# Loading x one piece at a time, and four semaphores for the first weight quarters, in an attention and feed-forward kernel on eight cores

## The chip, the cores and the metric

One Trainium2 chip, all eight of its cores. The batch has eight sequences and each core computes one of them by itself; the cores exchange nothing. The metric is the device time of the slowest core in microseconds. "Faster", "same" and "slower" go by a bound of 2%.

## The reference

```python
def _layernorm(x, axis=-1, eps=1e-5):
    m = jnp.mean(x, axis=axis, keepdims=True)
    v = jnp.var(x, axis=axis, keepdims=True)
    return (x - m) / jnp.sqrt(v + eps)

def attn(x, Wq, Wk, Wv, Wp):                 # 16 heads of 64, D = 1024
    q, k, v = x @ Wq, x @ Wk, x @ Wv         # split into heads
    scores = jnp.einsum('bnhk,bmhk->bhnm', q, k) / sqrt(64)
    out = jnp.einsum('bhnm,bmhv->bnhv', softmax(scores), v)
    return x + out @ Wp

def ffn(x, weight, aux_weight1, aux_weight2, bias):
    return jnp.tanh(x @ weight @ aux_weight1 @ aux_weight2 + bias)

x = x + attn(_layernorm(x), Wq, Wk, Wv, Wp)  # x: (8, 2048, 1024) f32
x = x + ffn(_layernorm(x), weight, aux_weight1, aux_weight2, bias)
```

## The kernel before

The host hands each core its sequence transposed, x as [1024, 2048] f32. On the chip `xr` holds it as eight chunks (j = 0 to 7) of 128 features by 2048 tokens, f32, 8 MB in all. The matrices are f32 in memory and are used as bf16; each is cut into four quarters of 256 output columns. A quarter is read as 1 MB of f32, cast on its way and written as 512 KB of bf16. GpSimd (POOL) issues these loads (`preload_head_quarters`, L170 to L175, and `issue_wdma`, L130 to L138). SyncE (SP) issues the loads of x (L210 to L212) and, much later, the stores of the result (L714). The two kinds of transfer thus stand in two queues, q0 for POOL and q1 for SP, and are moved by the same 16 DMA engines.

The work goes in stages.

1. Start. SP loads two identity matrices and the bias. All engines wait for these. POOL issues ten quarters in a row: the four of wq and the four of wk into the eight slots of `vt`, which is not needed for anything else yet, and the first two of wv into `wbuf`. SP issues four loads of x, 2 MB each, two chunks to a load: load jj fills chunks 2jj and 2jj + 1 and has a semaphore of its own, `d_x[jj]`.
2. Statistics of the first layer norm (L226 to L239). For each chunk VectorE (DVE) waits for its `d_x`, casts the chunk to bf16 (L231) and squares it (L233); TensorE (PE) then adds up values and squares over the features with eight matmuls against ones, four on `ln_mean` (L236) and four on `ln_sq` (L239). Casts use two buffers in turn, so a cast also waits for the matmuls of the chunk two before it.
3. When the last of these matmuls is done, DVE forms mean and variance over [128, 2048] (L244, L246, L248), ScalarE (ACT) takes Ln and Exp (L251, L253), and for each chunk DVE subtracts, multiplies and adds back (L261, L267, L271) while ACT casts the result to `S` (L269) and PE multiplies it with the first quarter of wq (L277).
4. Projections q and k (L327), v with transposes (L368, L392), a bound for the exponents (L424), and then the long attention loop, into which the output projection and the feed-forward network are woven.

A matmul that uses one of the first eight quarters (`use_wquarter`, L149 to L152) waits for a semaphore in `d_wh`. There are two of them: quarters 0, 2, 4, 6 count on the first and 1, 3, 5, 7 on the second, and the wait asks for all four of its semaphore.

```python
        for jj in range(4):
            d_x[jj].inc(SP.dma_start(xr_j[:, 2 * jj:2 * (jj + 1), :], xsrc[jj]))
...
                    if dma_gate:
                        VE.wait_ge(d_x[j // 2].h, 16)
                    if j >= 2:
                        VE.wait_ge(s_te.h, mm_mark[sl])
                    m1 = s_ve.inc(VE.tensor_copy(xbf[sl], src_f32_j[:, j, :]))
```

Of the kernel before, what the change touches and what calls it, by code (L numbers as in the profile page):

```python
# [51 lines left out]
def build_program(upto=99, dbg=False):  # L52
    nc = bass.Bass("TRN2", target_bir_lowering=False)
# [17 lines left out]
    E = ctx.enter_context  # L71
    with ctx:
# [32 lines left out]
        d_x = [DSem(E(nc.semaphore(f"d_x{i}"))) for i in range(4)]  # L105
        d_w = [DSem(E(nc.semaphore(f"d_w{i}"))) for i in range(NWS)]
        d_wf = [DSem(E(nc.semaphore(f"d_wf{i}"))) for i in range(6)]
        d_wh = [DSem(E(nc.semaphore(f"d_wh{i}"))) for i in range(2)]
        d_o = [DSem(E(nc.semaphore(f"d_o{i}"))) for i in range(2)]
        d_misc = DSem(E(nc.semaphore("d_misc")))  # L110

        TE, VE, SE, SP, GP = nc.tensor, nc.vector, nc.scalar, nc.sync, nc.gpsimd
# [15 lines left out]
        def wslot(s):  # L128
            return wbuf[:, 2048 * s: 2048 * (s + 1)].rearrange("p (i d) -> p i d", i=8)
# [10 lines left out]
        def vtslot(k):  # L140
            return vt.ap()[:, 2048 * k: 2048 * (k + 1)].rearrange("p (i d) -> p i d", i=8)
# [4 lines left out]
        def flslot(k):  # L146
            return kbslot(k) if k < 6 else vtslot(k - 6)

        def use_wquarter(idx):  # L149
            if idx < 8:  # L150
                TE.wait_ge(d_wh[idx % 2].h, 16 * 4)
                return vtslot(idx)  # L152
            if idx >= FLUSH_W0:
                k = idx - FLUSH_W0
                s = FL_SEM[k]
                nf = sum(1 for ss in FL_SEM if ss == s)
                TE.wait_ge(d_wf[s].h, 16 * nf)
                return flslot(k)
            s = idx % NWS
            nloads = sum(1 for i in range(8, idx + 1) if i % NWS == s)  # L160
            TE.wait_ge(d_w[s].h, 16 * nloads)
            return wslot(s)
# [7 lines left out]
        def preload_head_quarters():  # L170
            for k in range(8):
                wn, q = wq_order[k]
                src = w_d[wn].rearrange("(i p) d -> p i d",
                                        p=128)[:, :, 256 * q: 256 * (q + 1)]
                d_wh[k % 2].inc(GP.dma_start(vtslot(k)[:], src))  # L175

        def _fl_load(k):
            wn, q = wq_order[FLUSH_W0 + k]
# [20 lines left out]
        for e in (TE, VE, SE, SP):  # L199
            e.wait_ge(d_misc.h, d_misc.n)  # L200
        preload_head_quarters()
        issue_wdma(8)
        issue_wdma(9)
# [5 lines left out]

        xsrc = x_d.rearrange("(jj q p) n -> jj p q n", p=128, q=2)  # L210
        for jj in range(4):
            d_x[jj].inc(SP.dma_start(xr_j[:, 2 * jj:2 * (jj + 1), :], xsrc[jj]))  # L212

        def layernorm(src_f32_j, dst_bf16, add_back, dma_gate=False, wq0=False):
# [7 lines left out]
            with nc.psum_tensor(_nm("ln_mean"), [128, 2048], F32) as mps, \  # L222
# [31 lines left out]
                VE.wait_ge(s_se.h, m)  # L254
            def _normalize(wq0_pj):
                wsl0 = use_wquarter(0) if wq0_pj is not None else None
                mkq0 = 0
                for j in range(NCH):
# [49 lines left out]
        def wproj(widx0, src_bf, dst_bf, q0=0, ev_init=None):  # L308
            with nc.psum_tensor(_nm("pj0"), [128, 2048], F32) as p0, \
                 nc.psum_tensor(_nm("pj1"), [128, 2048], F32) as p1:  # L310
                pj = [p0, p1]
                ev_mark = [0, 0]
                first = True
                for q in range(q0, 4):
                    widx = widx0 + q
                    wsl = use_wquarter(widx)
                    for jj in range(2):
                        j = 2 * q + jj
                        sl = j % 2
                        if first and ev_init is not None:  # L320
                            TE.wait_ge(s_se.h, max(ev_init))
                        first = False
                        if ev_mark[sl]:
                            TE.wait_ge(s_se.h, ev_mark[sl])
                        for i in range(NCH):
                            for n4 in range(4):
                                ins = TE.matmul(  # L327
                                    pj[sl][:, 512 * n4:512 * (n4 + 1)],
                                    wsl[:, i, 128 * jj:128 * (jj + 1)],
                                    src_bf[:, 2048 * i + 512 * n4: 2048 * i + 512 * (n4 + 1)],  # L330
                                    start=(i == 0), stop=(i == NCH - 1))
                        mk = s_te.inc(ins)
                        SE.wait_ge(s_te.h, mk)
                        ev_mark[sl] = s_se.inc(SE.copy(dst_bf[:, 2048 * j:2048 * (j + 1)],
                                                       pj[sl][:]))
                        if jj == 1:
                            done_wquarter(widx, mk)
# [8 lines left out]
        with nc.psum_tensor("pva", [128, 1024], F32) as pva, \  # L346
# [11 lines left out]
            for q in range(4):  # L358
                widx = 8 + q
                wsl = use_wquarter(widx)  # L360
                for jj in range(2):
                    j = 2 * q + jj
# [502 lines left out]
def _get_nc():  # L865
    if "nc" not in _NC_CACHE:
        _NC_CACHE["nc"] = build_program()
    return _NC_CACHE["nc"]
# [31 lines left out]
```

## Time and profile before

| | us |
|---|---|
| median of 2 runs | 1317.65 (1317.57 to 1317.73) |
| the profiled execution, its own time | 1320.32 |
| its span, slowest core (core 1) | 1318.7 |
| spans of the eight cores | 1305.1 to 1318.7 |
| PE busy | 1009.0 (77%) |
| ACT busy | 723.9 (55%) |
| DVE busy | 413.2 (31%) |

The span runs from the first to the last instruction of one core. The profile shows the slowest core, core 1; the run's own time is 1.6 us more than its span, which lies around it. All times of the trace are counted from the span's start. Engines are PE, PEld (weight loads of PE), DVE, ACT, POOL and SP; a "q" behind a name means its sequencer, which issues transfers. A packet is one piece that a DMA engine moves; bytes are counted as written, so a weight quarter counts 512 KB.

### The profile page before, as it was taken

The numbers are of one execution on the slowest core, as the hardware profiler recorded it, in microseconds if no ns is written. First come the engines' busy times: TensorE is split into PE (matmuls) and PEld (weight loads), VectorE is DVE, ScalarE is ACT, GpSimd is POOL, SyncE is SP. The second block draws the span as 40 slices with busy tenths as digits, with TensorE's granted clock in tenths as the row PEclk, the third lists the DMA queues.
The fourth block names the chain that finished last, engine by engine and source line by source line (L and its number), as shares of the span: only waits on it lengthen the run. The fifth ranks groups of instructions, "written<-read, shape, count | busy, mean of one in ns | idle before, by whom it ended". The sixth has DMA issues, their size and how long they took to land.

```text
span 1318.7 us, 15346 instructions; the slowest of 8 cores (1305.1 to 1318.7 us)
## 1 busy us (share of the span) xinstructions
PE 1009.0 (77%) x5185; PEld 334.8 (25%) x5185; DVE 413.2 (31%) x542; ACT 723.9 (55%) x686; POOL 66.8 (5%) x80
## 2 busy tenths in 40 slices
PE   2345999886677777787997678799777879977676
PEld 1111444442122222222332222233222223322222
DVE  3596000345701101234222223522222342222354
ACT  0122222004588898298668729866872986677202
POOL 2000000000000000100110010011001001111100
PEclk9665999996599999899998889999888999988879
DMA  9900000121000000500453340045335004593901
GB/s 239 175 1 0 0 0 1 17 33 16 0 1 0 1 1 1 64 1 1 60 70 65 64 64 1 1 57 72 56 70 68 1 1 51 67 160 58 145 0 64
DMA packets 85113, 57.65 MB, mean 44 GB/s; under 512 B 2088, under 2 KB 79920, under 8 KB 84016
## 3 DMA queue, kind: packets, MB, share of 16 engines
q0 software_dynamic: 79040, 39.85, 24.6%
q1 hardware_dynamic: 6000, 16.82, 3.7%
q8 instruction: 46, 0.75, 0.2%
q14 instruction: 27, 0.22, 0.1%
HBM read 88.12 MB, written 8.39 MB: 73 GB/s over the span
## 4 chain that ended last, share of the span: by engine, by line
PE 43%; ACT 16%; DVE 6%; issue 5%; DMA 2%; ACTq 0%; DVEq 0%; POOLq 0%
ACT S L760 14%; PE sc L526 10%; PE pvs L772 9%; PE dns L782 6%; PE lnps L674 4%; PE wps L674 4%; PE wps L548 2%; PE lnps L692 2%; DMA wbuf<-wp 2%; PE lnps L548 2%; PE wps L692 1%; DVE S L793 1%; DVE S L795 1%; DVE S L655 1%; DVE vtmp L652 1%
## 5 line engine op out<-in xcount | busy, mean ns | idle before, releaser
L760 ACT ACTIVATE S<-sc,cbias 128x1024 bf16<-128x1024 f32 x512 | 550.9, 1110 | 191.7 <-PE dns L785 178.7
L526 PE MATMUL sc<-qb,kb 64*128 64x512 bf16 x512 | 202.1, 395 | 116.2 <-ACT S L760 106.9
L772 PE MATMUL pvs<-S,vt 128*64 128x512 bf16 x512 | 214.4, 419 | 25.9 <-DVE S L795 25.9
L777 PE MATMUL pvs<-S,vt 128*64 128x512 bf16 x512 | 215.1, 420 | 0.0
L530 PE MATMUL sc<-qb,kb 64*128 64x512 bf16 x512 | 206.1, 403 | 0.0
L785 PE MATMUL dns<-S,ones 128*64 128x512 bf16 x512 | 204.6, 400 | 0.0
L782 PE MATMUL dns<-S,ones 128*64 128x512 bf16 x512 | 204.5, 399 | 0.0
L526 PEld LDWEIGHTS sc<-qb,kb 64*128 64x128 bf16 x512 | 47.6, 93 | 342.2 <-issue 342.2
L327 PE MATMUL pj<-S,vt 128*128 128x512 bf16 x448 | 98.7, 384 | 6.3 <-ACT qb L294 3.9
L772 PEld LDWEIGHTS pvs<-S,vt 128*64 128x64 bf16 x512 | 55.1, 108 | 150.4 <-issue 150.3
L793 DVE COPY S<-pvs 128x512 f32<-128x512 f32 x32 | 22.1, 691 | 189.5 <-PE dns L785 189.5
L424 ACT ACTIVATE S<-qb 128x2048 bf16<-128x2048 bf16 x8 | 15.1, 1906 | 81.9 <-PEq L402 78.4
L327 PEld LDWEIGHTS pj<-S,vt 128*128 128x128 bf16 x448 | 44.1, 99 | 61.3 <-issue 9.8
L785 PEld LDWEIGHTS dns<-S,ones 128*64 128x64 bf16 x512 | 57.5, 112 | 0.0
L782 PEld LDWEIGHTS dns<-S,ones 128*64 128x64 bf16 x512 | 57.4, 112 | 0.1
L138 POOL DMA_DIRECT2D wbuf<-w x36 | 31.5, 874 | 510.1 <-PE sc L530 451.4
L777 PEld LDWEIGHTS pvs<-S,vt 128*64 128x64 bf16 x512 | 55.1, 108 | 0.0
L382 DVE CAST vtmp<-pva 128x1024 bf16<-128x1024 f32 x8 | 9.8, 1225 | 135.4 <-PE pva L368 135.4
L277 PE MATMUL pq0a<-S,vt 128*128 128x512 bf16 x32 | 14.9, 620 | 45.5 <-ACT S L269 45.5
L530 PEld LDWEIGHTS sc<-qb,kb 64*128 64x128 bf16 x512 | 47.6, 93 | 0.0
L548 PE MATMUL wps<-S,wbuf 128*128 128x512 bf16 x104 | 31.1, 453 | 20.5 <-DMA wbuf<-wp 15.1
L705 ACT ACTIVATE S<-S,bias_pp_sb 128x512 bf16<-128x512 bf16 x32 | 23.1, 722 | 37.2 <-DVE S L700 37.1
(153 smaller groups left out, 1123.8 us busy)
## 6 DMA issues: line engine op xcount, KB each, us to landing
wbuf<-w POOLq DMA_DIRECT2D x36, 512.0 KB, 6.2
xr<-x SPq DMA_DIRECT2D x4, 2048.0 KB, 24.0
out<-xr SPq DMA_DIRECT2D x32, 256.0 KB, 2.2
wbuf<-wp POOLq DMA_DIRECT2D x14, 512.0 KB, 6.4
vt<-w POOLq DMA_DIRECT2D x8, 512.0 KB, 20.0
vt<-wq POOLq DMA_DIRECT2D x4, 512.0 KB, 34.5
vt<-wk POOLq DMA_DIRECT2D x4, 512.0 KB, 48.6
wbuf<-wv POOLq DMA_DIRECT2D x4, 512.0 KB, 30.9
```

Of the source, the lines that this page charges most:

```text
L327: ins = TE.matmul(pj[sl][:, 512 * n4:512 * (n4 + 1)], wsl[:, i, 128 * jj:128 * (jj + 1)], src_bf[:, 2048 * i + 512 * n4: 2048 * i + 512 * ...
L526: TE.matmul(scs[sl][:, 0:512], kb[0:64, 2048 * p + 128 * m: 2048 * p + 128 * (m + 1)], qb[0:64, 2048 * p + 512 * c: 2048 * p + 512 * (c + 1)],
L530: ins = TE.matmul(scs[sl][:, 512:1024], kb[64:128, 2048 * p + 128 * m: 2048 * p + 128 * (m + 1)], qb[64:128, 2048 * p + 512 * c: 2048 * p ...
L548: ins = TE.matmul(acc[:], wsl[:, i, 128 * jj:128 * (jj + 1)], ao[:, 512 * i:512 * (i + 1)], start=(i == 0), stop=(i == NCH - 1))
L674: ins = TE.matmul(acc[:], wsl[:, i, 128 * jj:128 * (jj + 1)], rhs_of(i), start=(i == 0), stop=(i == NCH - 1))
L692: ins = TE.matmul(acc[:], wsl[:, i, 128 * jj:128 * (jj + 1)], h2st[:, 512 * i:512 * (i + 1)], start=(i == 0), stop=(i == NCH - 1))
L760: ins = SE.activation(p_un[sl], scs[sl][:], AF.Exp, bias=cbias[:], scale=0.125)
L772: TE.matmul(pvs[0:64, :], vt[:, 1024 * m + 128 * p: 1024 * m + 128 * p + 64], p_un[sl][:, 0:512], start=(m == 0), stop=(m == NM - 1), tile ...
L777: TE.matmul(pvs[64:128, :], vt[:, 1024 * m + 128 * p + 64: 1024 * m + 128 * (p + 1)], p_un[sl][:, 512:1024], start=(m == 0), stop=(m == NM ...
L782: TE.matmul(dns[0:64, :], ones64[:], p_un[sl][:, 0:512], start=(m == 0), stop=(m == NM - 1), tile_position=(0, 0), skip_group_check=True)
L785: ins = TE.matmul(dns[64:128, :], ones64[:], p_un[sl][:, 512:1024], start=(m == 0), stop=(m == NM - 1), tile_position=(0, 64), skip_group_ ...
L793: pv_evac_mark = s_ve.inc(VE.tensor_copy(ao_un, pvs[:]))
```

## The change

SP now waits, before it issues load jj of x, until load jj - 1 has landed. And the first eight quarters of weights count on four semaphores in place of two: quarter 0 alone on the first, quarter 1 alone on the second, 2, 4, 6 on the third and 3, 5, 7 on the fourth. No transfer, no instruction and no size is changed, and nothing changes its place on its engine.

```diff
-        d_wh = [DSem(E(nc.semaphore(f"d_wh{i}"))) for i in range(2)]
+        d_wh = [DSem(E(nc.semaphore(f"d_wh{i}"))) for i in range(4)]
+        WH_SEM = [0, 1, 2, 3, 2, 3, 2, 3]
...
         def use_wquarter(idx):
             if idx < 8:
-                TE.wait_ge(d_wh[idx % 2].h, 16 * 4)
+                s = WH_SEM[idx]
+                nh = sum(1 for ss in WH_SEM if ss == s)
+                TE.wait_ge(d_wh[s].h, 16 * nh)
                 return vtslot(idx)
...
-                d_wh[k % 2].inc(GP.dma_start(vtslot(k)[:], src))
+                d_wh[WH_SEM[k]].inc(GP.dma_start(vtslot(k)[:], src))
...
         for jj in range(4):
+            if jj:
+                SP.wait_ge(d_x[jj - 1].h, 16)
             d_x[jj].inc(SP.dma_start(xr_j[:, 2 * jj:2 * (jj + 1), :], xsrc[jj]))
```

SP's whole queue before, with what each entry waits for (`d_misc` counts the three small loads, `s_ve` is DVE's counter):

```order
L193 DMA identb_sb<-identb 128x128 [waits barrier_Pool_Activation_PE_DVE_SP_release]
L194 DMA identf_sb<-identf 128x8
L195 DMA bias_st<-bias 8x128
L212 DMA xr<-x 128x2x2048 [waits d_misc]
L212 DMA xr<-x 128x2x2048 x3
L714 DMA out<-xr 128x512 [waits barrier_Pool_Activation_PE_DVE_SP_release,s_ve]
L714 DMA out<-xr 128x512 [waits s_ve] x31
```

And after the change (lines are five further down):

```order
L196 DMA identb_sb<-identb 128x128 [waits barrier_Pool_Activation_PE_DVE_SP_release]
L197 DMA identf_sb<-identf 128x8
L198 DMA bias_st<-bias 8x128
L217 DMA xr<-x 128x2x2048 [waits d_misc]
L217 DMA xr<-x 128x2x2048 [waits d_x0]
L217 DMA xr<-x 128x2x2048 [waits d_x1]
L217 DMA xr<-x 128x2x2048 [waits d_x2]
L719 DMA out<-xr 128x512 [waits barrier_Pool_Activation_PE_DVE_SP_release,s_ve]
L719 DMA out<-xr 128x512 [waits s_ve] x31
```

The three last loads of x, which followed the first at once, each wait now for the one before them. On POOL, PE, DVE and ACT the rows are the same and stand in the same order.

## Rows read from the trace of the kernel before

**Rows 1.** The eight cores: span and mean granted clock; three of them.

```profile
core 1: 1318.7 us, clock 0.903
core 3: 1305.1 us, clock 0.913
core 7: 1306.0 us, clock 0.914
```

**Rows 2.** Timeline, 0 to 50 us: start, duration, instruction, idle time and its releaser.

```profile
4.50 2.96 SPq L212 DMA_DIRECT2D xr<-x  x4
...
8.64 1.83 POOL L138 DMA_DIRECT2D wbuf<-wv  x2
...
18.96 1.23 DVE L231 CAST qb<-xr 128x2048 bf16<-128x2048 f32 x1 [13.90 <-DMA xr<-x]
...
25.94 1.23 DVE L231 CAST qb<-xr 128x2048 bf16<-128x2048 f32 x1 [1.96 <-DMA xr<-x]
...
32.84 1.23 DVE L231 CAST qb<-xr 128x2048 bf16<-128x2048 f32 x1 [1.87 <-DMA xr<-x]
...
41.06 1.23 DVE L231 CAST qb<-xr 128x2048 bf16<-128x2048 f32 x1 [3.20 <-DMA xr<-x]
```

**Rows 3.** Timeline, 50 to 130 us.

```profile
50.43 2.29 DVE L244 TENSOR_SCALAR qb<-ln_mean 128x2048 f32<-128x2048 f32 x1 [4.35 <-PE ln_sq L239]
...
63.00 2.29 DVE L261 TENSOR_TENSOR qb<-xr,qb 128x2048 f32<-128x2048 f32 x1 [5.48 <-ACT qb L253]
...
69.83 1.86 PE L277 MATMUL pq0a<-S,vt 128*128 128x512 bf16 x4 [19.51 <-ACT S L269]
...
118.54 2.29 DVE L271 TENSOR_TENSOR xr<-xr,kb 128x2048 f32<-128x2048 f32 x1
...
128.01 7.24 PE L327 MATMUL pj<-S,vt 128*128 128x512 bf16 x25 [3.87 <-ACT qb L294]
```

**Rows 4.** The head's eight weight loads (L175): from issue to landing.

```profile
L175 POOL DMA_DIRECT2D vt<-wk x4: 923/938/950, 5.2 to 7.8; - x4
...
DMA to landing us min/median/max: 8.4/43.0/52.8
```

**Rows 5.** DMA queues, 20 to 26 us: packets, MB, share of 16 engines.

```profile
q1 hardware_dynamic: 246, 1.88, 90.6%
q0 software_dynamic: 243, 0.12, 14.9%
```

**Rows 6.** DMA queues, 46 to 54 us.

```profile
q0 software_dynamic: 2424, 1.22, 131.0%
```

**Rows 7.** Loads of x: who waited for them, and from issue to landing.

```profile
  DMA xr<-x: 20.9, 4
...
DMA to landing us min/median/max: 14.4/24.0/34.4
```

**Rows 8.** DMA queues, 4 to 8 us, and then 8 to 10 us.

```profile
q0 software_dynamic: 841, 0.43, 108.2%
...
q0 software_dynamic: 550, 0.27, 119.9%
q1 hardware_dynamic: 9, 0.07, 13.9%
```

**Rows 9.** Stores (L714), three stretches: 920 to 940, 1160 to 1180, 1212 to 1250 us.

```profile
DMA to landing us min/median/max: 2.2/2.2/2.2
...
DMA to landing us min/median/max: 6.1/6.4/6.7
...
L714 SPq DMA_DIRECT2D out<-xr x1: 332/332/332, 1218.8 to 1218.8; - x1
...
DMA to landing us min/median/max: 8.5/8.5/8.5
```

**Rows 10.** DMA traffic, 1218 to 1228 us in 40 slices of 0.25 us.

```profile
GB/s 14 25 80 174 197 195 186 184 197 195 180 162 123 139 123 145 160 184 123 80 139 178 217 264 299 252 240 205 203 193 115 148 166 152 147 135 131 131 147 180
```

**Rows 11.** Stages by time: PE busy (count), granted clock, DMA share, GB/s.

```profile
26.00:36.00 10.00, 5.57 (x26) 1.00 1.05 311
36.20:39.60 3.40, 3.40 (x10) 0.51 1.02 252
43.70:50.40 6.70, 6.56 (x16) 0.55 1.29 150
```

**Rows 12.** Longest waits of PE, 0 to 130 us: in total, times, longest.

```profile
PE pq0a L277 <- ACT S L269: 45.5, 8, 19.5
PE ln_mean L236 <- DVE qb L233: 24.2, 5, 16.9
```

**Rows 13.** Longest waits of SP's queue, whole span.

```profile
SPq L711 <- DVE xr L710: 946.9, 32, 337.5
```

## The prediction

> **What bounds the kernel now.** The change touches only the first 60 us, so I read the page for the whole, the list of cores, and then the timeline of the head, asking of each wait what ended it.
>
> The list of cores [rows 1] shows that the slowest core, 1, has the lowest granted clock (0.903); core 3, at 0.913, is 13.6 us shorter. That is the noise of size in this kernel, and the change has no direct hold on it.
>
> In the timeline DVE's casts L231 are the ones to look at. SP issues the four loads of x together at 4.50 us [rows 2]. DVE sits idle for the first until 18.96, and then again for the second, third and fourth: the casts start at 18.96, 25.94, 32.84 and 41.06, each with "DMA xr<-x" as releaser. So DVE waits for every load; the arrival of x sets the pace, and the intervals are 6.98, 6.90 and 8.22 us, 22.1 in all. Behind the last landing everything is a chain: statistics of two chunks until 50.43, mean and variance on DVE, Ln and Exp on ACT, the first subtraction at 63.00, the first projection matmul at 69.83, for which PE had waited 19.51 us [rows 3]. DVE's last operation of this chain is at 118.54, and no engine has other work it could do first. What is lost before 41.06 is therefore lost at the end, microsecond for microsecond.
>
> The weights are not on this chain. The last of the eight quarters is issued at 7.8 us and lands at most 52.8 us later [rows 4], at about 60.6, which is 9 us before PE first needs any of them, and then PE is released by ACT's cast, not by a DMA [rows 12].
>
> How do the two queues share the engines? Between 20 and 26 us, 246 packets of q1 (x) and 243 of q0 (weights) are moved: one for one, 1.88 MB against 0.12 [rows 5]. x has 313 GB/s and nearly the whole machine. When x is done, q0 alone moves 2424 packets in 8 us, 303 per us against 40 before [rows 6].
>
> The Trainium skill ("DMA: Bandwidth & Descriptors", section "Queues, rings and completion order") says that each engine takes turns between its queues packet by packet. By that rule, which these counts bear out, the big packets of x win whenever the queue of x is not empty. It would put the loss from the change in the times when that queue is empty, which is also what the rows below say.
>
> **The change part by part.**
>
> *The semaphores of the first quarters.* Before, the first projection matmul waits for quarters 0, 2, 4 and 6, now for 0 alone. All had landed 9 us earlier, so nothing is freed: 0 us. If x comes later, the matmul comes later too and the margin grows; the weights' own end moves by a few us at most (below). Both ends of this edit are 0; the cover is the late cast on ACT. The next quarters are used only from 128 us on [rows 3].
>
> *The waits on SP.* Three new waits. Behind the waiting instruction on SP stand only the next loads of x, and the stores, of which the first is issued at 694 us after SP has waited 337.5 us for DVE [rows 13]. So the waits hurt nobody but x itself. POOL issues from its own queue and doesn't see them.
>
> What a wait costs x: before, when an engine had moved its part of load jj, the packets of load jj + 1 stood behind it. Now its queue is empty until (a) all 16 engines have finished, (b) the semaphore has reached SP, (c) SP has issued the next load and its first packets come up. The price is the whole time from issue to landing of a load that starts into an empty queue, less the interval of a load that follows another. I look for rows of such a start.
>
> - The first load of x is one: same size, same queue, weights running beside it. Issued 4.50, landed after 14.4 us [rows 7]. And the queue rows show where that goes: from 4 to 8 us not one packet of q1, though issued; from 8 to 10 only 9, beside 550 of the weights [rows 8]. Some 4.8 us pass before x moves.
> - Stores of 256 KB, also on SP's queue. In a quiet stretch 2.2 us from issue to landing; beside a long row of weight loads 6.1, 6.7 and 8.5 [rows 9]. The slices show the last one: issued at 1218.79, and traffic rises above all that the weights had alone (197 GB/s) only in slices 23 to 27, from about 1223.5 on [rows 10]. Again about 4.7 us before the first packets.
>
> So two different transfers agree: with weights on the engines a start into the empty queue takes some 4.6 us to the first data. Add the 6.9 to 8.2 us of interval that a load needs once it flows, and 0.6 for the landing to be told (an estimate: a quiet store's 2.2 less 0.9 of data at 300 GB/s is 1.3, half of it ahead of the data and half behind). That is 12.1 to 13.4 us, and the whole first load says 14.4. I take 13.2, the middle of 12.1 and 14.4.
>
> Will weights be there in every gap? They have ten quarters, 5.24 MB, to write; by 19 us some 0.9 is done (0.43 and 0.27 to 10 us [rows 8], then 0.02 MB per us beside x [rows 5]). Each gap gives them about 4.6 us at 0.15 MB per us [rows 6], 0.7 MB, and each load leaves them about 0.2. At the third gap about 2.7 MB are done. They are still there, and end near 70 us (58.6 plus the last 1.6 MB at 0.15), the eighth quarter near 63.
>
> Sum: 3 x 13.2 = 39.6 us in place of 22.1, so x is complete 17.5 us later, at about 58.6. Does something absorb it? The pairs of chunks are 14 us apart instead of 7, and their 16 matmuls need 6.6 us at half speed [rows 11]; they are no bound. The last two chunks need 9.4 us behind the landing as before; their matmuls ran at a granted clock of 0.55, mostly the lower of the two levels. At full speed the 16 matmuls would end about 2 us sooner, but PE will have been idle longer before them than now, so I give it 0. The work behind is unchanged. On the profiled execution 1320.3 + 17.5 = 1337.8; the median of the runs is 2.7 us below the profiled time, so I predict 1317.65 + 17.5 = 1335.2.
>
> A bound below: quiet stores, 1.3 us of start and landing per load, +3 x 1.3 = +4, or -0 if a load has no uneven end any more. A bound above: 14.4 each, +21.1. Beyond it the longest store (8.5 against 2.2, +6.3 on top of 1.3) gives 6.9 + 7.6 = 14.5, the same.
>
> **The rivals.**
>
> *A quiet start.* The slow first start may belong to the start of the program, when POOL is still issuing loads (until 10.5 us [rows 2]) and all cores begin at once. Then a restart costs what a quiet store shows, 1.3 us, up to 2.2 if issue and landing hide nothing: +4 to +7, 1322 to 1325. For it: 9 packets come up just when POOL stops. Against it: the stores at 1168 and 1176 us, when POOL had long stopped issuing, also took 6 to 7 us.
>
> The Trainium skill (same page, section "Anatomy of one DMA") gives a fixed cost of about 2.0 us per DMA. By that rule the change costs 3 x 2.0 = 6 us and the time is 1323.7; the 2.2 of the quiet store agrees, the loaded stores do not.
>
> *Not slower at all.* Between 36 and 40 us x slows to 252 GB/s [rows 11], since some engines have finished their parts and others not. At 18.96 us some packets of load 2 have already gone, which the waits keep from load 1. If one load at a time has the engines evenly, each lands perhaps 1 us sooner, which pays the 1.3 us of a quiet restart, and with the last 16 matmuls at full clock 2 us come on top: 1316 to 1318. It decides where load jj + 1 lands within 7.4 us of load jj. Both must hold, a quiet restart and the gain; no row shows the second, so it is unlikely. It is also the case in which the waits do nothing, because the loads are taken in turn anyway.
>
> *Slower by over 2%*, over 1344.0. It needs +26.4 us: 14.4 per load (+21.1) and 5 us more, which a mean clock lower by 0.004 gives (13.6 us per 0.010, rows 1). Later x would have to change the clock of the attention; I see no path but chance, or a restart slower than the first.
>
> **How the numbers follow.** My forecast (restart beside running weights, +14 to +21.5) 0.70; quiet start 0.16; not slower 0.06; over 2% slower 0.07; and 0.01 for over 2% faster. 2% is about what a measurement of this kernel can tell from no change, and the forecast of 1.3% lies inside it: faster 0.01, same 0.92, slower 0.07. The range: my case with its spread (0.2% between the profiled execution and the median) reaches from 1329 to 1342; to leave no more than 2 in 10 out I take most of the quiet start in, from 1322.
>
> **What would show it.** In the changed kernel's timeline SP's loads of x stand apart, issued within 1 us of each landing. Casts of even chunks start at about 19, 32, 45 and 58.6 us; L244, 5 lines further down, at 68 in place of 50.4; the first projection matmul at about 87. DVE's wait for xr grows from 20.9 us in total [rows 7] to about 38. In the gaps the weights' packets rise to 300 per us, and the weights end near 70 us. From the last landing on, distances are as before. Wrong if the intervals are under 9 us (quiet start), if the first load lands clearly before 18, if PE waits for a DMA at the first projection, or if the head is as forecast and the end is not, which would put the time in the clock.

## The result, and the profile after

The changed kernel takes 1340.24 us (median of 11 runs) beside 1318.73 us for the kernel before (10 runs on the same chips). The ratio is 1.0153, with a 95% interval of 1.0124 to 1.0181: 16 to 24 us longer, about 20. It was forecast 17.5 us longer. In some runs of either kernel the cores of a die have a lower clock and take some per cent longer; the medians take these runs in, the ratios and the times of single runs leave them out. By the bound of 2% that is "same", and by the interval it is clearly slower.

The profiled execution has a span of 1336.0 us on core 0, now the slowest (before: 1318.7 on core 1). Its timeline from 15 to 90 us for DVE stands beside [rows 2, 3]; each line has start, duration, instruction, idle time before it and what ended that:

```profile
19.67 1.23 DVE L236 CAST qb<-xr 128x2048 bf16<-128x2048 f32 x1 [14.38 <-DMA xr<-x]
...
33.63 1.23 DVE L236 CAST qb<-xr 128x2048 bf16<-128x2048 f32 x1 [8.94 <-DMA xr<-x]
...
47.55 1.23 DVE L236 CAST qb<-xr 128x2048 bf16<-128x2048 f32 x1 [8.89 <-DMA xr<-x]
...
62.49 1.23 DVE L236 CAST qb<-xr 128x2048 bf16<-128x2048 f32 x1 [9.92 <-DMA xr<-x]
...
71.50 2.29 DVE L249 TENSOR_SCALAR qb<-ln_mean 128x2048 f32<-128x2048 f32 x1 [3.99 <-PE ln_sq L244]
84.07 2.29 DVE L266 TENSOR_TENSOR qb<-xr,qb 128x2048 f32<-128x2048 f32 x1 [5.48 <-ACT qb L258]
```

Read the last column. DVE still waits for every load of x, but behind the second, third and fourth it now idles 8.9, 8.9 and 9.9 us where it was 2 to 3. The intervals are 13.96, 13.92 and 14.94 us; they were 6.98, 6.90 and 8.22. From L249 on nothing has changed: 12.57 us to the first subtraction, as before, with the same 5.48 us for ACT in it.

The core shown is not the same as before, so the sum is better made over all eight. The statistics end (start of L244, now L249) at 48.5 us on average before and at 69.2 after. The projections (L327, now L332) begin at 126.1 and 146.7. Both say +20.7 us, which is the measured difference. Nearly all of it is in the intervals between the loads: from the first cast to that of the last load it is 21.7 us before and 41.2 after, on average, +19.5. Another 0.5 us comes from the first load and 0.7 from the work behind the last one. The loss is whole at 70 us and nothing behind takes it up.

The start of PE's projection waits for ACT as it did, not for a DMA. In the window from 69 to 92 us this row stands beside the third of [rows 3]:

```profile
90.90 1.44 PE L282 MATMUL pq0a<-S,vt 128*128 128x512 bf16 x3 [19.50 <-ACT S L274]
```

The price per load is in the landing times of core 0, to be held against [rows 7]. SP's second load is issued at 19.64 us, within 0.1 us of the landing of the first:

```profile
  DMA xr<-x: 42.1, 4
...
DMA to landing us min/median/max: 13.8/14.4/14.9
```

```profile
19.64 0.37 SPq L217 DMA_DIRECT2D xr<-x  x1
```

Before, the landing times ran from 14.4 to 34.4, since the later loads stood in line from 4.5 us on. Now all four take about as long as the first. The mean of the eight cores' medians is 13.9.

The queues of the changed kernel on core 0, first from 19 to 23 us (the gap), then from 24 to 31 us (the load); packets, MB, share of 16 engines. They are to be held against [rows 5, 6, 8]:

```profile
q0 software_dynamic: 1391, 0.70, 134.2%
q1 hardware_dynamic: 1, 0.00, 0.0%
...
q1 hardware_dynamic: 230, 1.87, 87.3%
q0 software_dynamic: 259, 0.13, 15.8%
```

The second load is issued at 19.64 us. From then to 23 us the engines move no packet of q1 and 1258 of the weights, 79 for each engine; the one packet of q1 in the window, of 4 bytes, comes before. The first packet of this load moves at 23.29 us, 3.65 us after the issue. Counted from the packets in the trace, over loads 2 to 4 of all eight cores, it is 3.9 us, in which each engine moves 81 weight packets. Then x flows, 33 packets per us, and the weights again get about one for one.

### The profile page after: what moved, and what is told of

Same layout as the page of the kernel before. It is cut to its first block, busy times and chain, and to the rows that moved or that the text cites. A ratio compares the mean times of both kernels' runs of the same rounds, so it can differ in the third digit from the quotient of the medians.

```text
span 1336.0 us, 15275 instructions; the slowest of 8 cores (1321.4 to 1336.0 us)
## 1 busy us (share of the span) xinstructions
PE 994.9 (74%) x5111; PEld 335.5 (25%) x5185; DVE 413.0 (31%) x542; ACT 723.2 (54%) x686; POOL 66.8 (5%) x80
## 4 chain that ended last, share of the span: by engine, by line
PE 42%; ACT 16%; issue 6%; DVE 6%; DMA 2%; ACTq 0%; DVEq 0%; POOLq 0%
ACT S L765 14%; PE sc L531 10%; PE pvs L777 9%; PE dns L787 6%; PE lnps L679 4%; PE wps L679 4%; PE wps L553 2%; PE lnps L697 2%; DMA wbuf<-wp 2%; PE lnps L553 2%; PE wps L697 1%; DVE S L800 1%; DVE S L798 1%; ACT S L710 1%; DVE S L660 1%
## 5 line engine op out<-in xcount | busy, mean ns | idle before, releaser
L790 PE MATMUL dns<-S,ones 128*64 128x512 bf16 x512 | 202.5, 396 | 0.0
L787 PE MATMUL dns<-S,ones 128*64 128x512 bf16 x512 | 202.4, 395 | 0.0
L332 PE MATMUL pj<-S,vt 128*128 128x512 bf16 x439 | 98.2, 383 | 6.8 <-ACT qb L299 3.9
L798 DVE COPY S<-pvs 128x512 f32<-128x512 f32 x32 | 22.1, 691 | 189.6 <-PE dns L790 189.6
L332 PEld LDWEIGHTS pj<-S,vt 128*128 128x128 bf16 x448 | 44.1, 99 | 61.3 <-issue 9.8
## 6 DMA issues: line engine op xcount, KB each, us to landing
xr<-x SPq DMA_DIRECT2D x4, 2048.0 KB, 14.4
```

What stands on the lines that cost most here:

```text
L332: ins = TE.matmul(pj[sl][:, 512 * n4:512 * (n4 + 1)], wsl[:, i, 128 * jj:128 * (jj + 1)], src_bf[:, 2048 * i + 512 * n4: 2048 * i + 512 * ...
L787: TE.matmul(dns[0:64, :], ones64[:], p_un[sl][:, 0:512], start=(m == 0), stop=(m == NM - 1), tile_position=(0, 0), skip_group_check=True)
L790: ins = TE.matmul(dns[64:128, :], ones64[:], p_un[sl][:, 512:1024], start=(m == 0), stop=(m == NM - 1), tile_position=(0, 64), skip_group_ ...
L798: pv_evac_mark = s_ve.inc(VE.tensor_copy(ao_un, pvs[:]))
```

## The experiments

Each diff is against the kernel that the text names. "Per load" is the time from issue to landing, as the median of a core's four loads, averaged over the eight cores: 13.9 us in the changed kernel.

**The two edits apart.** e1 has only the semaphores:

```diff
-            if jj:
-                SP.wait_ge(d_x[jj - 1].h, 16)
```

> Only the four semaphores, no waits on SP. My theory: nothing, ratio 1.000 within the interval, casts of x at about 19, 26, 33 and 41 us, first projection matmul at about 70 released by ACT. Rival (the semaphores carry part of the 20 us, say by another order of landing): 1.003 or more.

Measured 1.0008 (0.9984 to 1.0032). On the slowest core the casts at 18.24, 25.24 and 39.89 us are released by the DMA, as before, and the one at 32.39 by PE; the statistics end at 47.06 us. e2 is the kernel before with nothing but the waits:

```diff
+            if jj:
+                SP.wait_ge(d_x[jj - 1].h, 16)
```

> Only the waits on SP, with the two semaphores of before. My theory: the whole loss, ratio 1.013 to 1.018, loads of x 13 to 15 us from issue to landing, statistics done at 67 to 71 us. Rival (the semaphores carry a part): under 1.012.

Measured 1.0164 (1.0142 to 1.0187). Loads land after 13.7 to 14.0 us. The whole loss is in the waits, and no effect of the semaphores can be told.

**One load kept in line.** e3, against the changed kernel:

```diff
-            if jj:
-                SP.wait_ge(d_x[jj - 1].h, 16)
+            if jj >= 2:
+                SP.wait_ge(d_x[jj - 2].h, 16)
```

> Load jj of x waits for load jj - 2 in place of jj - 1, so one load always stands behind the one that moves. My theory (the price is the start into an empty queue, 4.6 us each): the loads follow each other every 7 to 8 us again, ratio 0.998 to 1.003. Rival (each wait costs its issue and its notice, whatever is queued): two waits cost 2 to 4 us, ratio 1.002 to 1.003, and gaps show at loads 3 and 4. Second rival (the loads lose bandwidth to the weights as soon as fewer than four are queued): intervals of 9 us and more, ratio over 1.005.

Measured 0.9996 (0.9982 to 1.0009). Its DVE timeline, slowest core:

```profile
19.26 1.23 DVE L236 CAST qb<-xr 128x2048 bf16<-128x2048 f32 x1 [14.19 <-DMA xr<-x]
...
26.03 1.23 DVE L236 CAST qb<-xr 128x2048 bf16<-128x2048 f32 x1 [1.75 <-DMA xr<-x]
...
33.25 1.23 DVE L236 CAST qb<-xr 128x2048 bf16<-128x2048 f32 x1 [2.12 <-PE ln_sq L244]
...
40.54 1.23 DVE L236 CAST qb<-xr 128x2048 bf16<-128x2048 f32 x1 [2.27 <-DMA xr<-x]
```

The intervals are 6.8, 7.2 and 7.3 us: two waits on SP at no cost that can be told, as long as one load still stands behind the one that moves. So it is not the wait nor the issue that costs, but the queue running empty. That the weights might take bandwidth when fewer than four loads are queued falls too.

**What a start waits for.** If it is the weights' packets ahead of it, the wait must shrink to that of a quiet start without weights. e5, against the changed kernel:

```diff
+        GP.wait_ge(d_x[3].h, 16)
         preload_head_quarters()
         issue_wdma(8)
```

> The changed kernel, and POOL issues no weights until the last load of x has landed. So every load of x starts into empty queues on engines that nobody uses. My theory (the dear part of a start is waiting behind the weights' packets): a start costs what a quiet store shows, about 1.3 us, loads land 8 to 9.5 us after their issue, x is complete at 38 to 43 us, and the kernel is within 0.5% of before. Rival (a start after a pause costs 4.6 us by itself): 12 to 14 us per load, x complete at 55 to 60, ratio 1.010 or more.

Measured 0.9974 (0.9962 to 0.9986): with all three waits in it, slightly faster than the kernel before, since its first load no longer has weights beside it either: the first cast starts at 13.1 us on average, before it was 18.5. Core 4, loads of x, and below it core 0's queue from 14 to 18 us, in the middle of the second load:

```profile
DMA to landing us min/median/max: 8.4/9.1/9.6
```

```profile
q1 hardware_dynamic: 208, 1.67, 99.4%
```

8.2 us per load on average over the cores, and 51 packets of x per us while one flows. The first packet of loads 2 to 4 comes 1.5 us after the issue, so the rival that a start costs 4.6 us by itself is out. The waits aren't free on quiet engines, though. e7 below is the same kernel without them: there the statistics end at 39.9 us on average, here at 45.5. That is 5.6 us for three waits, 1.9 each.

Is it the transfer that an engine has begun? e4 loads each of the head's eight quarters in two halves (PE's waits count twice as much):

```diff
-                d_wh[WH_SEM[k]].inc(GP.dma_start(vtslot(k)[:], src))
+                for hf in range(2):
+                    d_wh[WH_SEM[k]].inc(GP.dma_start(vtslot(k)[:, 4 * hf:4 * hf + 4, :],
+                                                     src[:, 4 * hf:4 * hf + 4, :]))
```

> The changed kernel with each of the first eight weight quarters loaded by two transfers of 256 KB, so 32 or 33 packets for each DMA engine in place of 65. It asks what x waits for at a start: if it is the rest of the weight transfer that an engine has begun (65 packets at 19 per us are 3.4 us), the time from issue to the first packet of x falls from about 4.6 to about 2.9 us and a load lands after 12 to 13 us in place of 14.4; if it is a fixed number of packets that the engines have taken ahead, or a cost of the start itself, it stays at 4.6 and 14.4.

14.0 us per load, and 1342.48 us in its one run: no change, so halving the transfers doesn't matter while all are queued. Then the number that stands ahead was varied. e6 takes e4 and issues a half only when the one before has landed:

```diff
                 for hf in range(2):
+                    if prev[0] is not None:
+                        GP.wait_ge(prev[0].h, prev[0].n)
+                    prev[0] = d_wh[WH_SEM[k]]
...
+        GP.wait_ge(d_wh[3].h, d_wh[3].n)
         issue_wdma(8)
```

> The changed kernel with the first eight weight quarters in sixteen halves, each issued only when the one before has landed, so no more than 33 weight packets stand on an engine at any time. If a load of x must first see out the packets that stand ahead on each engine, and these are at most 33, its first packet comes 3 us after issue or sooner and it lands after 11 to 12.5 us. If the mere presence of weight traffic costs 4.6 us, it stays at 14.

9.3 us per load, under what was expected. Its one run took 1316.5 us, beside a median of 1318.63 for the kernel before. e8 and e9 give each quarter its own semaphore and let one or two whole quarters be in flight. This is e8; e9 has `k >= 2` and `d_q[k - 2]`:

```diff
+                if k >= 1:
+                    GP.wait_ge(d_q[k - 1].h, 16)
+                d_q[k].inc(GP.dma_start(vtslot(k)[:], src))
...
+        GP.wait_ge(d_q[7].h, 16)
         issue_wdma(8)
```

> The changed kernel with a semaphore for each of the first eight quarters, and each quarter issued only when the one before has landed: at most 65 weight packets stand on an engine, twice as many as in e6. If x waits for what stands ahead of it up to a fixed number, the time from issue to the first packets lies between e6's and the changed kernel's, 2 to 4.5 us depending on how far the quarter has got, and the loads land after 10.5 to 13 us. If one weight transfer in flight at a time is what helped in e6 and not its size, it is as e6, under 10.

> As e8, but a quarter waits for the one before the last, so two are in flight, 65 to 130 packets on an engine. If the number that is taken ahead is bounded (the halves of e4 say that it is not the transfer), the start costs about what it does in the changed kernel, 4 to 4.6 us, and loads land after 13 to 14.5 us. If it isn't bounded but grows with all that is queued, it costs clearly less than there, under 12.5 us a load.

Core 5 of e8 and core 7 of e9, loads of x:

```profile
DMA to landing us min/median/max: 11.0/11.5/13.3
```

```profile
DMA to landing us min/median/max: 11.0/12.9/13.6
```

e8's loads are within what was expected, though their first packets come after 1.7 us, sooner than the 2 to 4.5 expected. e9's 12.9 us lies between its two cases, 13 or more and under 12.5. The table has all together. The last two columns are counted from the packets in the traces, as means over loads 2 to 4 of the eight cores:

| weight packets on an engine, at most | kernel | us per load | issue to first packet | first packet to last |
|---|---|---|---|---|
| 0 | e5 | 8.2 | 1.5 | 6.3 |
| 33 | e6 | 9.3 | 1.4 | 7.3 |
| 65 | e8 | 11.1 | 1.7 | 8.7 |
| 130 | e9 | 12.9 | 2.1 | 9.6 |
| all | e4 | 14.0 | 3.8 | 9.5 |
| all | changed kernel | 13.9 | 3.9 | 9.4 |

The more weight packets may stand there, the longer a load of x takes to land, and the single times rise with it: 1316.5 (e6), 1326.4 (e8), 1332.6 (e9) and 1342.5 us (e4). The last two columns say that these are two effects. Up to one quarter in flight the start is about as quick as on quiet engines, and nearly the whole difference is in the flow. The long start shows only with all quarters queued. From e5 to the changed kernel the start gives 2.4 us and the flow 3.1.

The chained kernels change two things at once. They leave fewer packets ahead of x, and they also leave x alone for part of each load: on core 0 of e8 the engines move 8 weight packets from 9 to 13 us, while the first load flows. No run here separates the two. The last load of e9 finds the weights nearly done; its loads 2 and 3 alone have 2.3 us to the first packet and 10.2 from first to last.

**The other way round.** If weights ahead make x late, they also make its first load late, in the kernel before too. e7 is the kernel before with the four semaphores and e5's gate on POOL, without waits on SP:

```diff
+        GP.wait_ge(d_x[3].h, 16)
         preload_head_quarters()
         issue_wdma(8)
```

> The kernel of before with the four semaphores and without the waits on SP; POOL issues no weights until the last load of x has landed. My theory: the first load of x too is freed of the weights ahead of it and lands after 9 to 10 us in place of 14.4, the loads behind it every 6.5 us, x is complete at 33 to 35 us in place of 41, the first quarter lands by 42, before the first projection at about 62; ratio 0.993 to 0.996. Rival (the start of the program is slow by itself): first load 14 us, x complete near 38, ratio 0.997 to 0.999. Second rival: the weights, now late, are waited for by PE, and the time is that of before or longer.

Measured 0.9935 (0.9917 to 0.9953), median 1309.47 us. By the ratio it is 8.6 us shorter than the kernel before, and so faster than both kernels. The statistics end 8.6 us earlier as well, at 39.9 us on average where it was 48.5. The slowest core, DVE, and PE's longest waits from 0 to 130 us (beside [rows 12]):

```profile
15.07 1.23 DVE L235 CAST qb<-xr 128x2048 bf16<-128x2048 f32 x1 [9.92 <-DMA xr<-x]
...
33.75 1.23 DVE L235 CAST qb<-xr 128x2048 bf16<-128x2048 f32 x1 [0.70 <-DMA xr<-x]
40.91 2.29 DVE L248 TENSOR_SCALAR qb<-ln_mean 128x2048 f32<-128x2048 f32 x1 [2.14 <-PE ln_sq L243]
```

```profile
PE pq0a L281 <- ACT S L273: 45.5, 8, 19.5
PE ln_mean L240 <- DVE qb L237: 18.6, 7, 12.9
```

x is complete at 33.75 instead of 41.06 (each on its slowest core), and though the weights now start behind it, PE waits for none of them.

Only there could the semaphores matter. e10 is e7 with the two semaphores of before.

> e7 with the two semaphores of before: the first projection matmul now waits for quarters 0, 2, 4 and 6, and these are issued from 34 us on. At 3.5 us a quarter the seventh lands at about 34 + 5 + 23 = 60 to 62 us, and the matmul is wanted at about 60. My theory: it waits 0 to 3 us for the DMA on some cores, ratio 0.993 to 0.996, within the intervals as e7. Rival (the semaphores matter once the weights are late): PE waits over 4 us there and the gain shrinks to 0.997 or more.

Measured 0.9929 (0.9909 to 0.9948), not to be told from e7. PE did wait, on core 0, window 55 to 66 us:

```profile
64.94 1.44 PE L278 MATMUL pq0a<-S,vt 128*128 128x512 bf16 x3 [24.83 <-DMA vt<-wk]
```

The matmul starts at 64.94, some 5 us after it could have, but it is one of eight such groups that DVE releases every 7.2 us and that take 3.7 us, so PE has caught up by the third, which starts at 74.06 us and waits for ACT again. The wait of over 4 us came, as the rival had it, and the loss that it drew from it did not.

**Smaller pieces of x.** e11 is e7 with eight loads of one chunk (and eight `d_x`, POOL waiting for the last):

```diff
-        xsrc = x_d.rearrange("(jj q p) n -> jj p q n", p=128, q=2)
-        for jj in range(4):
-            d_x[jj].inc(SP.dma_start(xr_j[:, 2 * jj:2 * (jj + 1), :], xsrc[jj]))
+        xsrc = x_d.rearrange("(j p) n -> j p n", p=128)
+        for j in range(8):
+            d_x[j].inc(SP.dma_start(xr_j[:, j, :], xsrc[j]))
...
-                        VE.wait_ge(d_x[j // 2].h, 16)
+                        VE.wait_ge(d_x[j].h, 16)
```

> e7 with x in eight loads of one chunk (1 MB, a semaphore each) in place of four of two. All eight stand in the queue from the start, so no load starts into an empty queue and x is complete at the same 33 to 34 us; but the last but one chunk is there some 3 us earlier, and behind the last landing only one chunk is cast, squared and added up. My theory: the statistics end 2 to 3 us earlier than in e7 (41 us), ratio 0.991 to 0.993. Rival (smaller loads move slower, or SP's issue of eight holds the first ones back): as e7 or longer, 0.994 and more.

Measured 0.9926 (0.9913 to 0.9939), 1306.71 us. The slowest core:

```profile
33.48 1.23 DVE L235 CAST qb<-xr 128x2048 bf16<-128x2048 f32 x1 [0.34 <-DMA xr<-x]
38.18 2.29 DVE L248 TENSOR_SCALAR qb<-ln_mean 128x2048 f32<-128x2048 f32 x1 [2.14 <-PE ln_sq L243]
```

The last chunk lands as in e7 and the statistics end 2.4 us sooner (mean of the cores 37.5 against 39.9). The trace shows the 2 to 3 us; the ratio's interval overlaps with e7's, so the time alone doesn't.

## Why the prediction was right

- *The semaphores, 0 us.* Right within 0.3%: e1, and e10 even where the margin is gone.
- *Nobody but x stands behind the waits.* Right: the whole loss is in e2, and the head's +20.7 us is the time's +20.
- *The price of a load, 13.2 us in place of 6.9.* As an interval from cast to cast it is 13.7 us on average, so this term was a little small, three times 0.5 us. Its parts were off by more, in opposite ways, and that the sum came so near is partly luck. The start was put at 4.6 us and takes 3.9. The flow was put at 6.9 to 8.2, the interval of a load that stands in line, and takes 9.4 from first packet to last.
- *The other 1.7 us between 17.5 and 20.7.* The 22.1 us of before were those of core 1; the mean of the cores is 21.7. The first load was put as unchanged and its cast starts 0.5 us later. The work behind the last landing was put as unchanged too, from core 1's 9.4 us; the mean of the cores went from 8.3 to 9.1.
- *Weights in every gap.* Right: 1391 packets in four microseconds.
- *Nothing absorbs it.* Right. Most of the last 16 matmuls ran at the lower level again (granted clock 0.59 from 65.5 to 71.5 us on core 0): DVE waits 3.99 us for them, before it was 4.35 [rows 3].
- *The quiet start* (0.16) is what e5 would be: right for an empty chip, 8.2 us, and wrong for this one. The Trainium skill ("DMA: Bandwidth & Descriptors", section "Anatomy of one DMA") would have had 3 x 2.0 = 6 us; the section gives that figure for transfers that GpSimd issues. e5 and e7 agree with a cost of that kind for SP's loads, 5.6 us for three waits, and the changed kernel, at 20 us, does not. What told them apart ahead of the run were the three stores beside weight loads, 6.1 to 8.5 us [rows 9].
- *Not slower at all* and *over 2% slower* did not happen. The profiled execution has a mean span of the cores only 16.4 us longer, where the head grew by 20.7, as if the attention loop gave some back. It doesn't: over the runs behind the ratios the mean span is 1329.5 us in e2 and 1308.7 for the kernel before on the same chip, +20.8, and 1330.5 in the changed kernel. The mean granted clock is lower, 0.905 in e2 against 0.913. On core 0 that shows in the head, 0.78 from 0 to 90 us against 0.83 from 0 to 70 before; in the 1230 us behind, it is 0.91 to 0.92 in both (cores 0, 1 and 4).

## What to carry to other kernels

A load that sets the pace should never find its own queue empty while another queue keeps the same engines busy: keep at least one behind it (e3 cost nothing that can be told), or keep the other queue's transfers few or late. Ask of each early transfer when its data is first used; here 5 MB of weights, first needed at 70 us, stood ahead of the x that everything waited for, and holding them back gained 8.6 us. For the price of a restart, take a row with the same neighbours on the engines, not a quiet one: 2.2 us against 6 to 8.5 for the same store. And take a whole load that starts alone, not a start plus the interval of a load in line.

## What the runs showed of the hardware

- A load that starts into an empty queue while another queue has many transfers waiting sees its first packet after 3.9 us, against 1.5 on quiet engines. Each engine moves 81 weight packets in these 3.9 us, and 81 to 86 where the weight transfers are half as large (e4), so it isn't the rest of one transfer. With at most one quarter outstanding it is 1.4 to 1.7 us. That speaks for a bounded number taken ahead by each engine; such a store of packets was not seen, and no run fixes its size.
- Once it flows, a lone load of 2 MB takes 6.3 us from first packet to last on quiet engines and 9.4 beside the weights.
- Beside the weights, x moved 267 GB/s with one load queued (24 to 31 us above) and 313 with several [rows 5]. In packets of 8 KB that is 33 and 38 per us: the 246 of [rows 5] hold 16 of 4 bytes. By this difference a load of the changed kernel takes about 1 us longer (an estimate, 256 packets at either rate). Without weights it was the other way: 51 per us for a single load in its middle (e5), 41 with more queued (below, 15 to 33 us of e7). The cause of both is open; what the other cores load at the same time was not varied.

```profile
q1 hardware_dynamic: 784, 6.05, 97.5%
```
